# Two attention and feed-forward blocks on one core: gate and up products in float32r with x in two parts, aggregated row moments, and a new order of the chunk stages

## What is computed

```python
x = x + attn_a(layernorm(x))      # 16 heads of 8, softmax over all 1024 keys
x = x + ffn(layernorm(x))
x = x + attn_b(layernorm(x))      # the same, with a causal mask
x = x + ffn(layernorm(x))         # the same integer weights again

def layernorm(x, eps=1e-5):
    return (x - mean(x)) / sqrt(var(x) + eps)       # over the 128 numbers of a row

def ffn(x):                       # w_gate, w_up: 384x128, w_down: 128x384, int32 in -127..127
    gate = x @ (w_gate / 127).T
    up   = x @ (w_up / 127).T
    return (silu(gate) * up) @ (w_down / 127).T
```

## Time and profile before

| | us |
|---|---|
| median of 3 runs | 1463.46 |
| lowest and highest run | 1460.33, 1463.71 |
| the profiled execution | 1464.76 |
| its span, as the trace has it | 1462.5 |

### The profile page before, as it was taken

The page is one execution under the profiler, slowest core; times in us unless marked ns, Lnnn a source line. Parts: engine busy times, 40 slices in busy tenths (PEclk is TensorE's granted clock), DMA queues, the critical chain, the costliest instruction groups (busy, mean ns, idle before and its releaser), DMA issues.

```text
span 1462.5 us, 26609 instructions
## 1 busy us (share of the span) xinstructions
PE 1374.2 (94%) x9625; PEld 683.6 (47%) x9625; DVE 1226.2 (84%) x3106; ACT 1001.4 (68%) x1771; POOL 94.4 (6%) x178
## 2 busy tenths in 40 slices
PE   2699999999999999999999997999999999999888
PEld 2454444444444444444435664555555555554465
DVE  7599999999999999999916767788888888886454
ACT  4518888888888888888884441577677777767422
POOL 6002000000000000000001110200000000000000
PEclk9859999999999999999999995799999999999999
DMA  3621111101111111011000232122112112110001
GB/s 103 200 75 30 31 30 31 26 12 24 31 30 31 30 31 31 19 18 26 2 1 30 91 91 79 31 46 46 32 37 55 31 32 60 32 31 3 8 22 29
DMA packets 40058, 58.41 MB, mean 40 GB/s; under 512 B 7796, under 2 KB 19448, under 8 KB 39928
## 3 DMA queue, kind: packets, MB, share of 16 engines
q1 hardware_dynamic: 39928, 56.72, 16.5%
HBM read 36.77 MB, written 18.87 MB: 38 GB/s over the span
## 4 chain that ended last, share of the span: by engine, by line
PE 82%; DVE 8%; ACT 5%; issue 2%; DMA 1%; SPq 1%; POOL 1%; DVEq 0%; ACTq 0%; POOLq 0%
PE psum L924 26%; PE psum L876 24%; PE psum L890 15%; PE psum L989 5%; DVE maxima L703 4%; PE psum L819 4%; ACT probs L498 4%; PE psum L994 3%; PE psum L829 2%; PE psum L898 2%; DVE xn L624 1%; PE psum L941 1%; DVE junk L700 1%; DMA k_parts<-parts 1%; ACT ot L528 1%
## 5 line engine op out<-in xcount | busy, mean ns | idle before, releaser
L498 ACT ACTIVATE probs<-psum 128x512 f32<-128x512 f32 (+3 forms) x1408 | 833.6, 658 | 216.4 <-PE psum L890 116.3
L703 DVE TENSOR_REDUCE maxima<-psum 128x1 f32<-128x512 f32 x1280 | 805.1, 682 | 20.5 <-PE psum L876 15.0
L876 PE MATMUL psum<-kop,qop 62*128 62x512 f32 (+3 forms) x1792 | 592.4, 449 | 18.0 <-DVE v L643 11.1
L890 PE MATMUL psum<-qop,kop 64*128 64x512 f32 (+3 forms) x1792 | 527.1, 422 | 6.4 <-ACT probs L498 2.5
L876 PEld LDWEIGHTS psum<-kop,qop 62*128 62x128 f32 x1792 | 283.7, 192 | 402.7 <-DVE maxima L703 299.0
L924 PE MATMUL psum<-probs,v 128*32 128x512 f32 (+3 forms) x3584 | 440.4, 564 | 0.6 <-ACT probs L498 0.5
L890 PEld LDWEIGHTS psum<-qop,kop 64*128 64x128 f32 x1792 | 268.7, 187 | 76.1 <-ACT probs L498 45.3
L700 DVE CUSTOM_DVE_ANT_0 junk<-psum,mask 128x384 bf16<-128x384 f32 (+3 forms) x512 | 233.5, 485 | 50.3 <-PE psum L876 46.5
L924 PEld LDWEIGHTS psum<-probs,v 128*32 128x32 f32 x3584 | 70.9, 108 | 101.0 <-issue 67.5
L898 PE MATMUL psum<-half_ident,key_mask 64*128 64x64 bf16 x1024 | 89.7, 197 | 0.0
L989 PE MATMUL psum<-ffn_xt,wffn 128*128 128x512 f32 x192 | 89.2, 603 | 0.0
(11 more groups left out here) (87 smaller groups left out, 679.5 us busy)
## 6 DMA issues: line engine op xcount, KB each, us to landing
qop<-q_parts SPq DMA_DIRECT2D x256, 64.0 KB
q_parts<-parts SPq DMA_DIRECT2D x32, 256.0 KB, 3.0
k_parts<-parts SPq DMA_DIRECT2D x32, 256.0 KB, 3.4
kop<-k_parts SPq DMA_DIRECT2D x64, 128.0 KB
kop<-k_parts SPq DMA_DIRECT2D x128, 64.0 KB
x<-in_L_attn_a_x SPq DMA_DIRECT2D x8, 256.0 KB, 4.3
qop<-shift_rows SPq DMA_DIRECT2D x128, 8.0 KB
out_x<-x SPq DMA_DIRECT2D x8, 256.0 KB, 2.3
```

The lines of the kernel that those rows point to most:

```text
L498: nc.scalar.activation(probs[:, slot, heads[0] % 2:heads[-1] % 2 + 1, c0:], psum[:, bank:bank + len(heads), c0:], ACT.Exp, scale=SCORE_SCA ...
L703: nc.vector.tensor_reduce(dst, src, AX_X, ALU.max).then_inc(ring_free, 1)
L876: mm(psum[:, bank, 0:width], qop[rows, buf, f, r, qb * P:(qb + 1) * P].bitcast(F32R), kop[rows, buf, r, kh * CHUNK:kh * CHUNK + width].bit ...
L890: ins = mm(psum[:, bank + k, c0:], kop[rows, buf, c // 2, j * P:(j + 1) * P].bitcast(F32R), qop[rows, buf, f, c // 2, c0:].bitcast(F32R), ...
```

## The change

The diff has four parts.

- **Gate and up in float32r.** The integer weights of gate and up are kept as integers (`gate_up_w`, float32r, not scaled). The transposed input `ffn_xt` is kept in two parts: ACT copies PSUM to part 0 with rounding to float32r, and DVE subtracts part 0 from PSUM into part 1 (`split_ffn_xt`, a new operation, with a new semaphore `ffn_low_ready`). Each gate or up product is two float32r matmuls, one per part, into the same bank. The scale 1/127 moves into `silu` for gate; for up it moves into the down weights, which are scaled by 1/127 twice. PE waits for `ffn_low_ready` where it waited for `xt_ready[1]`.
- **Row moments by aggregation.** The seven small DVE operations give way to one `bn_aggr` per tile. The epsilon is added on POOL by an operation of its own, with a wait (`guarded`) between it and the power.
- **Order on DVE.** `add_projection` moves ahead of the normalisation of chunk m and is parted from the row moments that follow it (`projected_moments`); in layer 1 the feed-forward is added to x after those moments and no longer at the top of the turn; `split_chunk` is parted into `add_v` and `split_qk` with the new `split_ffn_xt` between.
- **Order on PE and ACT.** PE runs `transpose_ffn_xn` before all of `down` and no longer before its last six halves; ACT runs `copy_ffn_xt` before the cast of q and k in `take_qk` and no longer after it.

```diff
             def inverse_deviation(k, mo, count):
                 pool.wait_ge(var_ready[k], count)
-                nc.gpsimd.tensor_tensor(mo[:, 1], mo[:, 5], power[:, 0:mo.shape[-1]], ALU.pow).then_inc(rstd_ready[k], 1)
+                nc.gpsimd.tensor_scalar(mo[:, 1], mo[:, 1], EPS, None, ALU.add).then_inc(guarded[k], 1)
+                pool.wait_ge(guarded[k], count)
+                nc.gpsimd.tensor_tensor(mo[:, 1], mo[:, 1], power[:, 0:mo.shape[-1]], ALU.pow).then_inc(rstd_ready[k], 1)
...
-            def take_qk(layer, g, buf, banks):
+            def take_qk(layer, g, buf, banks, between=None):
...
+                if between:
+                    between()
                 act.wait_ge(qk_ready, 2 * (g + 1))
                 wait(act, parts_stored[buf], (g - buf) * (STORES // 2))
                 nc.scalar.copy(parts[:, buf, 0].bitcast(F32R), qk[:, buf]).then_inc(part1_ready, 1)
...
-                    nc.scalar.copy(ffn_xt[:], psum[:, bank, :]).then_inc(xt_ready[1], 1)
+                    nc.scalar.copy(ffn_xt[:, 0].bitcast(F32R), psum[:, bank, :]).then_inc(xt_ready[1], 1)
...
-                    nc.scalar.activation(hid[:, c, :], psum[:, 2 + 2 * (c % 2), :], ACT.Silu).then_inc(silu_ready, 1)
+                    nc.scalar.activation(hid[:, c, :], psum[:, 2 + 2 * (c % 2), :], ACT.Silu, scale=DEQUANT).then_inc(silu_ready, 1)
...
                     if qkv_stage:
                         copy_xt(g + CHUNKS, buf, 1)
-                        take_qk(1, g + CHUNKS, buf, 4)
-                    if out_stage:
+                        take_qk(1, g + CHUNKS, buf, 4, (lambda: copy_ffn_xt(n + 2, 0)) if out_stage else None)
+                    elif out_stage:
                         copy_ffn_xt(n + 2, 0)
...
-                s = st.rearrange("p t s -> p s t")
-                dve.wait_ge(moment_steps[k], 3 * count + 1)
-                nc.vector.tensor_tensor(mo[:, 2], s[:, 1], s[:, 4], ALU.add)
...
-                nc.vector.tensor_tensor(mo[:, 5], mo[:, 3], mo[:, 4], ALU.add).then_inc(var_ready[k], 1)
+                dve.wait_ge(moment_steps[k], count + 1)
+                for t in range(tiles):
+                    ins = nc.vector.bn_aggr(mo[:, 0:2, t], st[:, t, :])
+                ins.then_inc(var_ready[k], 1)
...
-            nc.vector.tensor_scalar(wflt, wint, DEQUANT, None, ALU.mult).then_inc(wflt_ready, 1)
+            nc.vector.tensor_copy(wflt[:, 0:2], wint[:, 0:2])
+            nc.vector.tensor_scalar(wflt[:, 2], wint[:, 2], DEQUANT * DEQUANT, None, ALU.mult).then_inc(wflt_ready, 1)
...
+                def split_ffn_xt(n, bank):
+
+                    dve.wait_ge(xt_ready[1], layer * CHUNKS + n + 1)
+                    nc.vector.tensor_tensor(ffn_xt[:, 1].bitcast(F32R), psum[:, bank, :], ffn_xt[:, 0], ALU.subtract).then_inc(ffn_low_ready, 1)
...
-                    if residual_stage:
+                    def add_ffn():
                         dve.wait_ge(down_psum, g + 1)
                         add_to_x(n, 7, x_new)
+
+                    if residual_stage and layer == 0:
+                        add_ffn()
                     if qkv_stage:
                         dve.wait_ge(x_new, g + 1)
                         dve.sem_inc(begun, 1)
...
                     if ffn_stage:
                         gate(0)
+                    if out_stage:
+                        add_projection(n + 2)
                     if qkv_stage:
                         dve.wait_ge(rstd_ready[0], g + 1)
                         normalise(0, n, moments[:, buf], 0, xn[:, buf], g + CHUNKS - 1)
                     if out_stage:
-                        add_projection(n + 2)
+                        projected_moments(n + 2)
+                    if residual_stage and layer == 1:
+                        add_ffn()
                     if ffn_stage:
                         gate(1)
                         gate(2)
...
-                        split_chunk(1, n, buf, 1)
+                        add_v(1, n, buf, 1)
+                    if out_stage:
+                        split_ffn_xt(n + 2, 0)
+                    if qkv_stage:
+                        split_qk(g + CHUNKS, buf)
...
                     pe.wait_ge(ot_ready, g + 1)
-                    wait(pe, xt_ready[1], g)
+                    wait(pe, ffn_low_ready, g)
                     transpose_tiles(ot, bank).then_inc(ot_psum, 1)
...
                         for k in range(2):
-                            mm(psum[:, 2 + 2 * (c % 2) + k, :], wffn[:, k, c, :], ffn_xt[:], start=True, stop=True).then_inc(gate_up_psum, 1)
+                            for part in range(PARTS):
+                                ins = mm(psum[:, 2 + 2 * (c % 2) + k, :], gate_up_w[:, k, c, :].bitcast(F32R),
+                                         ffn_xt[:, part].bitcast(F32R), start=part == 0, stop=part == PARTS - 1)
+                            ins.then_inc(gate_up_psum, 1)
...
                         qkv_products(1, g + CHUNKS, buf, 4, 1)
+                    if out_stage:
+                        transpose_ffn_xn(n + 2, 0)
                     if ffn_stage:
                         pe.wait_ge(hid_ready, FB * (g + 2))
                         wait(pe, x_new, g + 1)
-                        down(range(TPC - 1))
-                    if out_stage:
-                        transpose_ffn_xn(n + 2, 0)
-                    if ffn_stage:
-                        down(range(TPC - 1, TPC)).then_inc(down_psum, 1)
+                        down().then_inc(down_psum, 1)
```

More of the change, by code:

```diff
@@ L167, in transformer_pair_kernel @@
         ffn_xn = sb("ffn_xn", [P, TPC, E], F32)
-        ffn_xt = sb("ffn_xt", [P, CHUNK], F32)
+        ffn_xt = sb("ffn_xt", [P, PARTS, CHUNK], F32)
         qk = sb("qk", [P, 2, 2, CHUNK], F32)
@@ L223, in transformer_pair_kernel @@
         var_ready = [sem(f"var_ready{k}") for k in range(3)]
+        guarded = [sem(f"guarded{k}") for k in range(3)]
         rstd_ready = [sem(f"rstd_ready{k}") for k in range(3)]
@@ L253, in transformer_pair_kernel @@
         x_mid = sem("x_mid")
+        ffn_low_ready = sem("ffn_low_ready")
         gate_up_psum = sem("gate_up_psum")
@@ L557, in _ @@
                         act.wait_ge(setup_psum, 2 + k)
-                        nc.scalar.copy(wffn[:, k].rearrange("p c d -> p (c d)"), psum[:, k, 0:HIDDEN]).then_inc(setup_ready, 1)
+                        dst = gate_up_w[:, k].bitcast(F32R) if k < 2 else down_w[:]
+                        nc.scalar.copy(dst.rearrange("p c d -> p (c d)"), psum[:, k, 0:HIDDEN]).then_inc(setup_ready, 1)
                 for kind, w, number, what in plan.walk:
@@ L633, in add_to_x, with add_v @@
                                         ALU.add).then_inc(done, 1)
-            def split_chunk(layer, n, buf, v_bank):
+            def add_v(layer, n, buf, v_bank):
                 g = layer * CHUNKS + n
@@ L644, in split_chunk, with split_qk @@
                 ins.then_inc(v_ready, 1)
+            def split_qk(g, buf):
                 dve.wait_ge(part1_ready, g + 1)
@@ L680, in first_chunk @@
                     normalise(0, n + 2, first_moments, (n + 2) * TPC, xn[:, buf], n + 1)
-                split_chunk(0, n, buf, 4 + 3 * buf)
+                add_v(0, n, buf, 4 + 3 * buf)
+                split_qk(n, buf)
             pipeline(dve, first_chunk)
             dve.wait_ge(other_weights_loaded, 5 * SEM_DMA)
-            nc.vector.tensor_scalar(wflt, wint, DEQUANT, None, ALU.mult).then_inc(wflt_ready, 1)
+            nc.vector.tensor_copy(wflt[:, 0:2], wint[:, 0:2])
+            nc.vector.tensor_scalar(wflt[:, 2], wint[:, 2], DEQUANT * DEQUANT, None, ALU.mult).then_inc(wflt_ready, 1)
             for layer, plan in enumerate(PLANS):
@@ L727, in add_projection, with projected_moments @@
                     add_to_x(n, 6, x_mid)
+                def projected_moments(n):
+                    g = layer * CHUNKS + n
                     dve.wait_ge(x_mid, g + 1)
@@ L742, in early_chunk @@
                         add_projection(0)
+                        projected_moments(0)
                         normalise_rows(0)
+                    if i == plan.project_at[2]:
+                        split_ffn_xt(0, 4)
                 unscaled, unnegated = [], []
@@ L988, in gate_up, with down @@
                         for k in range(2):
-                            mm(psum[:, 2 + 2 * (c % 2) + k, :], wffn[:, k, c, :], ffn_xt[:], start=True, stop=True).then_inc(gate_up_psum, 1)
-                    def down(tiles):
-                        for t in tiles:
+                            for part in range(PARTS):
+                                ins = mm(psum[:, 2 + 2 * (c % 2) + k, :], gate_up_w[:, k, c, :].bitcast(F32R),
+                                         ffn_xt[:, part].bitcast(F32R), start=part == 0, stop=part == PARTS - 1)
+                            ins.then_inc(gate_up_psum, 1)
+                    def down():
+                        for t in range(TPC):
                             for c in range(FB):
```

(2 more changed lines are left out.)

17 lines of the change are left out of this document (5 added, 12 removed).

## The result

The changed kernel takes 1468.62 us in the median of 20 runs (1459.64 to 1473.31), the kernel before 1463.38 in 20 runs beside it (1459.22 to 1466.74). The ratio is 1.0033, with a 95% interval of 1.0023 to 1.0044: 5.2 us slower, just past the 0.3% that the prediction takes as telling a change from none. The profiled execution after has a span of 1467.3 us, before 1462.5.

What follows compares the result with a forecast made beforehand. PE was taken to set the turn in both layers. From 1464.76, less 11.0, less 6.2, plus 1.0 gave 1448.6; clock falls of 13.2 and 6.6 gave 1468.4; the median 1.3 lower: 1467 us, range 1447 to 1484.

Steps and rivals of the forecast that it cites:

- What bounds before: Chunk stages: PE sets the turn in both layers, 14.41 and 11.48 us; DVE has 3.7 us slack in layer 0.
- Gate and up: Chunk stages: a float32r product takes 0.23 us, a pair 0.46, a chunk 2.8 instead of 5.2 on PE.
- the rival at 0.44: Gate and up: a float32r product on all rows takes 0.44 us, so PE keeps its work; 1465, chance 0.05.
- The split: Splitting ffn_xt adds one DVE operation of 0.69 us behind add_v, with split_qk waiting behind it.
- Moments: Chunk stages: four bn_aggr take 0.40 us where seven operations took 0.77; POOL's extra operation costs 0.30.
- the wait for POOL: Layer 0's turn: DVE waits 0.15 us for POOL's step before it normalises.
- The rival of 0.20 each: Moments: bn_aggr costs as much as bn_stats, 0.20 us; 1480 with clock falls, 1460 without; chance 0.07.
- The two sums: Chunk stages at full clock: layer 0 gains 11 us with turns of 12.76, layer 1 gains 6.2 with 10.84.
- Start: Start of the kernel: 24 aggregations and POOL's extra step make it 1.0 us later, between 0 and 3.9.
- The clock: PE's new gaps: six falls in layer 1, three in layer 0, 2.2 us each, costing 13.2 and 6.6.
- That the clock holds: Both chunk stages: the clock stays at 1.00 through the new gaps, 1447 us; chance 0.25.
- That it falls in every gap of both layers: Both chunk stages: fourteen falls at 2.8 us, 39 us in all, give 1486; chance 0.13.

Runs made afterwards that it cites:

- Aggregation alone: The kernel before with only the row moments changed to bn_aggr, old products and old order: 1461.00 us, ratio 0.9994.
- the run with more fillers: Changed kernel with unused TensorE products in its waits in both layers, none in layer 1's last turn, 18 and 2 in layer 0's last: 1445.48 us.
- with fillers: Changed kernel with extra TensorE products, overwritten unused, put where TensorE waits in the chunk stages of both layers: 1446.72 us, ratio 0.9890.
- float32r alone: The kernel before with only gate and up in float32r on rows split in two parts, old moments and old order: 1467.33 us, ratio 1.0029.

## Why the prediction was right, step by step

The forecast of 1467 us lies 1.6 under the measured median, and the mechanism in it is the one that the runs show: at full clock the two stages gain about 17 us, the start gives 1 of it back, and the falls of the clock take more than the rest. That the number came out so close is in part luck, as the terms below show, and the direction was never sure: the forecast gave 0.36 to faster and 0.41 to slower.

*What bounds before* held. Aggregation alone moved no turn, so DVE had slack there.

*Gate and up.* Forecast 0.46 for a pair of parts; four products with the last one's drain take 1.17, eight 2.09, so 0.23 each and 0.46 for a pair. The price taken from products on half the rows is that of products on all rows; the rival at 0.44 is out.

*The split* took 0.69, behind `add_v`, as forecast.

*Moments.* Forecast 0.40 for four; the operation itself shows 0.38, but the next one on DVE starts 0.29 behind the first, where the old seven held it 0.77. The term was too dear by about 0.1. The turns had been forecast at 12.76 and 10.84 and took 12.59 and 10.61 at full clock. In layer 0, where two aggregations stand in the chain, this is 0.2; the wait for POOL, 0.30 where 0.15 stood, takes most of that back, and steps of a few hundredths make up the rest of the 0.17. In layer 1 it is 0.1 of the 0.23; the moved add and the two gates, 1.77 (1398.13 to 1399.90 above) where 1.95 stood, are the larger part. The rival of 0.20 each is out.

*The two sums.* With the clock held, layer 0's stage went from 105.88 to 95.38, 10.5 less where 11 stood. The six turns gave 10.9 instead of 9.9, but the first turn became 0.9 longer (8.13 for 7.26, the transposes wait for DVE there as in layer 1) and the last one 0.4 shorter (11.75 for 12.16), where the forecast had the two 1.0 shorter together. The sum of 11 was nearly met because these errors cancel. Layer 1's went from 85.76 to 78.83 in the run with more fillers, 6.9 less where 6.2 stood.

*Start.* Forecast 1.0; in the kernel after, from the first operation behind bn_stats to POOL's power it is 2.23 (29.83 to 32.06 below), where it was 1.17: 1.06 more. The timeline of the start:

```profile
29.83 1.69 DVE L617 BATCH_NORM_AGGREGATE first_moments<-first_stats 128x2 f32<-128x6 f32 x24
31.69 0.28 POOL L399 TENSOR_SCALAR first_moments<-first_moments 128x24 f32<-128x24 f32 x1 [6.69 <-DVE first_moments L617]
32.06 4.19 POOL L401 TENSOR_TENSOR first_moments<-first_moments,power 128x24 f32<-128x24 f32 x1
```

The first job came at 73.61 instead of 72.40, but between the other kernels with aggregation it lies anywhere from 72.4 to 74.5, so the stage as a whole doesn't show 1.0.

*The clock.* Forecast nine falls at 2.2, 19.8 us. Measured, as the difference of the stages to those at full clock: layer 0 103.80 less 95.38, 8.4, in five falls of 1.6 to 1.7 each; layer 1 91.91 less 78.83, 13.1, in seven falls: 1.3 to 1.7 each, but 2.8 and 2.9 in the two turns where the clock stays low longer (mean clock 0.75, as in the window from 1398.13, and not 0.86). That is 21.5 in twelve falls: more of them, and cheaper, 1.8 in the mean, near the lower bound of 1.67 that the earlier trace rows gave; some lie below it, so it was no bound. The two errors nearly cancel, and that is luck: no row of before could tell twelve falls from nine. Layer 0 was mis-sized most, five falls where three stood. Together: less 10.5, less 6.9, plus 1.1, plus 21.5 is 5.2 more, and the medians differ by 5.2; with the walks moving by 1 to 2 us, so exact an agreement is chance.

*The rivals.* That the clock holds was priced at 1447; with fillers the kernel takes 1446.7. That it falls in every gap of both layers was priced at 1486: in layer 1 it does, in layer 0 not, and a fall costs 1.8 in the mean. The Trainium skill (TensorE: Matmul & The Clock Gate, Loop structure matters more than you think) says that a loop's nest decides the clock. Layer 1's turns agree, with seven falls in seven, which the trace of before could not show; layer 0's don't, since of six middle turns of one nest three fell and three did not. The same section of the Trainium skill shows a loop in which DVE's reading of PSUM leaves the clock up, since TensorE has the next tile to work on; here the wait of 3.16 us for DVE's rows at 1401 brought it down, because what stood next in TensorE's order needed those rows.

*What the working missed* did not move the forecast. It treated the new order as one thing, paid for in layer 1 by a gap that it sized nearly rightly (3.6 forecast, 3.2 measured). It did not ask what layer 1 would do with the other two parts in the old order: 10.05 a turn and no falls. In layer 0 the order is needed (14.57 with float32r alone, 13.21 with the order); in layer 1 it costs 15.5 us (91.91 against 76.42).

## What to carry to other kernels

When an engine is relieved until another one sets the pace, price its new waits twice: as time, and by the clock at which the work behind them runs; the windows and the length of one known product (here the down product, 2.84 or 5.33) tell the two apart. An order that helps one loop need not be carried into its sister loop: try it per loop, and look at which DVE step stands ahead of the one that TensorE waits for. Where a wait can't be shortened, overwritten products in a free PSUM bank can hold the clock (here 21.9 us), and cost nothing as long as they end before the wait does; in layer 1's last turn, where they did not, they cost 1.5 us.

## What the runs showed of the hardware

The clock's loss hangs on small differences. In layer 1 a wait of 1.54 us in every middle turn left the clock at 1.00; with waits of 2.0 to 2.2 it fell in three or four of five middle turns, with waits of 3.2 in all. In layer 0 the same wait of 1.05, in turns of the same instructions, was followed by a fall in some turns and not in others (the lines at 799.46 and 813.74). I can't give a bound from this, and the runs don't settle what tells such turns apart.

The walk of layer 1 begins at half clock even though TensorE is 0.82 to 0.96 busy in the first four windows of 10 us, and when the clock comes back differs from one execution to the next. Windows of 10 us from the first job, the fourth and the fifth, first with the fillers in both layers, then with more of them:

```profile
909.24:919.24 10.00, 9.56 (x70) 5.39 (x70) 7.46 (x29) 6.39 (x9) 6.93 (x3) 0.75 0.52 100
919.24:929.24 10.00, 10.00 (x89) 4.86 (x86) 8.47 (x30) 8.57 (x11) 0.10 (x1) 1.00 0.06 8
```

```profile
906.50:916.50 10.00, 9.56 (x62) 6.12 (x62) 6.70 (x27) 5.99 (x8) 6.60 (x1) 0.50 0.53 100
916.50:926.50 10.00, 10.00 (x67) 4.08 (x66) 6.33 (x21) 6.67 (x8) 0.44 (x2) 0.71 0.06 8
```

In the first the clock rises some 10 us earlier, and the walk to the next projection's add is 3.4 us shorter (462.8 and 466.2 from the first job). The other traces show that this is no effect of the fillers. In the eight profiled kernels with aggregation the clock comes back either 35 to 36 us after that first job (five of them, 462.6 to 463.0 from the job to the add) or 46 us after it (three, 466.1 to 466.3). Two executions so differ by 3 us in work that is all but the same. This can hide what the extra fillers saved in the last turn of layer 0. What decides between the two cases stays open, and I did not try to hold the clock there.

Aggregating is cheap beside taking the statistics: 24 in 1.69 us, 0.07 each, where bn_stats took 0.20 each.
